# Large transfers issued from ScalarE's queue, and thirteen more attention chunks turned by DMA, in a layer kernel on one core

## What is computed

```python
xn = _layernorm(x, axis=-1)
# attention: one head, causal, with a linear bias on the distance
scores = einsum('bqe,bke->bqk', xn @ W_qk, xn) * SCALE + (kpos - qpos) * alibi_slope[0]
s = softmax(where(causal, scores, -inf)) @ (xn @ W_v.T)
# mixture of experts: 8 experts, 512 slots each, the best expert of a token alone
probs = softmax(xf @ Wr); eidx = argmax(probs); rank = place of the token in its expert
h = maximum(xe @ W1[e], 0); ye = (h @ W2[e]) * p_tok       # xe: the rows sent to expert e
x = x + s * _silu(y)
```

## Time and profile before

| | |
|---|---|
| median of 3 runs | 438.6 us (438.42 to 440.61) |
| the profiled execution, own time | 441.75 us |
| its span | 440.0 us |
| PE busy | 420.4 us, 96% |
| DVE busy | 322.4 us, 73% |
| ACT busy | 222.7 us, 51% |
| POOL busy | 228.3 us, 52% |
| DMA | 76.01 MB, mean 173 GB/s |

### The profile page before, as it was taken

The page is one execution under the profiler, slowest core; times in us unless marked ns, Lnnn a source line. Parts: engine busy times, 40 slices in busy tenths (PEclk is TensorE's granted clock), DMA queues, the critical chain, the costliest instruction groups (busy, mean ns, idle before and its releaser), DMA issues.

```text
span 440.0 us, 8367 instructions
## 1 busy us (share of the span) xinstructions
PE 420.4 (96%) x3015; PEld 288.6 (66%) x3015; DVE 322.4 (73%) x838; ACT 222.7 (51%) x444; POOL 228.3 (52%) x353
## 2 busy tenths in 40 slices
PE   6899999998999899999989999999999999999996
PEld 2667576756668676766666666666666666665666
DVE  5989778988888478778747787979796967424553
ACT  3755454452657146545424555545455545454551
POOL 3257851826544826056102566575757576757530
PEclk9999999999999999999999999999999999999999
DMA  7996898366945634266866577676888873234840
GB/s 238 294 294 151 277 295 191 74 130 163 279 90 111 139 115 117 57 216 153 120 96 232 165 245 226 205 250 176 281 156 280 179 206 98 90 120 113 159 98 31
DMA packets 104280, 76.01 MB, mean 173 GB/s; under 512 B 73263, under 2 KB 98108, under 8 KB 102192
## 3 DMA queue, kind: packets, MB, share of 16 engines
q1 hardware_dynamic: 92976, 53.11, 47.3%
q0 software_dynamic: 5824, 16.74, 12.9%
q10 hardware_dynamic: 5440, 5.64, 3.9%
HBM read 31.33 MB, written 28.58 MB: 136 GB/s over the span
## 4 chain that ended last, share of the span: by engine, by line
PE 64%; DVE 13%; DMA 11%; issue 4%; ACT 4%; POOL 1%; SPq 1%; another core or an unknown queue 0%; ACTq 0%; POOLq 0%; DVEq 0%
PE bank L1419 18%; PE bank L1421 18%; PE bank L1420 17%; DMA xg<-in_x 4%; DMA pT<-p_rows 3%; PE bank L1510 3%; DVE sc L1012 3%; PE bank L1513 3%; PE bank L1512 3%; PE bank L1491 2%; ACT sc L1269 2%; DVE p_rows L1033 2%; DMA rows<-xg 1%; DMA slots<-xnr,slot_idx 1%; DMA xeT<-slots 1%
## 5 line engine op out<-in xcount | busy, mean ns | idle before, releaser
L1510 PE MATMUL bank<-v_h,pT 128*128 128x257 f16 x272 | 74.7, 274 | 3.2 <-DMA pT<-p_rows 3.2
L1513 PE MATMUL bank<-v_h,pT 128*128 128x257 f16 x272 | 74.1, 272 | 0.0
L1512 PE MATMUL bank<-v_l,pT 128*128 128x256 f16 x272 | 73.7, 271 | 0.0
L1296 ACT ACTIVATE hid_h<-bank 128x512 f16<-128x512 f32 x64 | 38.1, 596 | 67.7 <-PE bank L1421 59.8
L1102 DVE SCALAR_TENSOR_TENSOR hid_l<-bank,hid_h 128x512 f16<-128x512 f32 x64 | 44.0, 688 | 38.0 <-ACT hid_h L1296 33.7
L1421 PE MATMUL bank<-w_h,hid_l 128*128 128x256 f16 x256 | 69.8, 273 | 0.0
L1419 PE MATMUL bank<-w_h,hid_h 128*128 128x256 f16 x256 | 69.8, 273 | 0.0
L1420 PE MATMUL bank<-w_l,hid_h 128*128 128x256 f16 x256 | 69.8, 273 | 0.0
L1012 DVE CUSTOM_DVE_ANT_0 sc<-bank,bias,score_mul 128x512 f32<-128x512 f32 (+2 forms) x80 | 52.9, 664 | 9.1 <-PE bank L1421 9.0
L1419 PE MATMUL bank<-xT,qT_h 128*128 128x512 f16 (+3 forms) x160 | 55.0, 347 | 3.1 <-DVE cmin L1012 1.7
L1285 ACT ACTIVATE pT<-bank 128x512 f16<-128x512 f32 (+3 forms) x50 | 24.6, 494 | 60.3 <-PE bank L1491 50.9
(11 more groups left out here) (198 smaller groups left out, 919.9 us busy)
## 6 DMA issues: line engine op xcount, KB each, us to landing
raw<-in_w_e SPq DMA_DIRECT2D x5, 2048.0 KB
sc<-in_w_e SPq DMA_DIRECT2D x3, 2048.0 KB
slots<-empty ACTq DMA_DIRECT2D x1, 4224.0 KB, 18.7
gates<-gate SPq DMA_DIRECT2D x8, 512.0 KB
out<-xg SPq DMA_DIRECT2D x7, 512.0 KB
rows<-xg SPq DMA_DIRECT2D x7, 512.0 KB, 7.2
rows<-so SPq DMA_DIRECT2D x7, 512.0 KB
xg<-in_x SPq DMA_DIRECT2D x6, 512.0 KB, 4.4
```

The lines of the kernel that those rows point to most:

```text
L1296: a_.activation(hid_h[:, f % HB, :], sc_ps[f % 2][:, :], ACT.Relu).then_inc(h_hi, 1)
L1510: pe.matmul(pv_ps[t % 2][:, 0:D + 1], p_h, v_h[:, at, q, 0:D + 1], start=kb == 0, stop=False)
L1512: pe.matmul(pv_ps[t % 2][:, 0:D], p_h, v_l[:, at, q, :], start=False, stop=False)
L1513: last = pe.matmul(pv_ps[t % 2][:, 0:D + 1], p_l, v_h[:, at, q, 0:D + 1], start=False, stop=kb == t % NT)
```

## The change

- Three buffers `p_rows` instead of two, the third in two blocks of `hid_h`, which the experts fill later.
- Thirteen more chunks by DMA: chunk 0 of tiles 4 to 7 and of 12 to 14; in the second sequence chunk 0 of 20, 21, 22, chunks 0 and 1 of 23, and chunk 0 of 27. `pT_in` is one semaphore per parity of the tile and chunk.
- `group_out`, `group_in`, `group_s` from group 1 or 2 on and the two weight loads of the main loop are issued from ScalarE, at the end of a step given by a table.
- A group's four turns are placed one by one after chunk turns (`turns_after`): groups 2 and 3 still after tiles 3 and 6, group 4 in tile 11, 5 in 15, 6 in 16, 7 in 21 and 22.
- Units of group 7: values in tile 23's first two steps, its rank at the end of tile 24 instead of the first step of 25. The second expert's rows are asked for after the loop.

```diff
-        p_rows = [sb(f"p_rows{k}", [P, GT, 2, P], F16) for k in range(2)]
+        p_rows = [sb(f"p_rows{k}", [P, GT, 2, P], F16) for k in range(NX - 1)]
+        p_rows += [hid_h[:, HB - 2:HB, :].rearrange("p f t -> p (f t)").rearrange("p (b h t) -> p b h t", b=GT, h=2)]
...
-            if t in (REST - 1, TILES - 1):
+            if chunk_blocks(t, c) < GT:
                 return False
-            if chunks(t) == 4:
-                return c == 1 if t == NT - 1 else c in ((1, 2) if t < NT else (0, 1, 2))
-            return chunks(t) == 3 and c < 2
+            if t < NT:
+                return c == 1 if t == NT - 1 else c in {2: (0,), 3: (0, 1), 4: (0, 1, 2)}.get(chunks(t), ())
+            return c in {REST - 1: (0,), TILES - 1: ()}.get(t, range(chunks(t)) if t >= NT + GT else ())
...
-                   REST - 5: [VAL, VAL + 1] * last,
-                   REST - 4: [VAL + 2, VAL + 3] * first + [PICK] * (c == 1),
-                   REST - 3: [RANK] * first,
+                   REST - 5: [VAL, VAL + 1] * first + [VAL + 2, VAL + 3] * (c == 1),
+                   REST - 4: [PICK] * (c == 1) + [RANK] * last,
...
+        def turns_after(t, c):
+
+            if t in (3, 6):
+                return [(t // 3 + 1, j) for j in range(GT) if last_step(t, c)]
+            if t == 11:
+                return [(4, j) for j in range(GT) if min(j, 2) == c]
+            if t in (NT - 1, NT):
+                return [(t - 10, c)]
+            if t in (REST - 7, REST - 6) and c < 2:
+                return [(LATE, (t - REST + 7) * 2 + c)]
+            return []
+
...
-        SECOND_LOAD = 23
+        FIRST_LOAD, SECOND_LOAD = (6, 0), (23, 1)
+        OUT_AT = {(4, 0): 2, (8, 0): 3, (10, 0): 4, (12, 0): 5, (17, 0): 6}
+        IN_AT = {(5, 1): 2, (9, 0): 3, (11, 1): 4, (13, 2): 5}
+        S_AT = {(6, 1): 0, (9, 2): 1, (13, 0): 2, (18, 0): 3, (21, 1): 4, (25, 1): 5}
...
                 for c in steps(t):
                     if by_dma(t, c):
                         chunk_turn(t, c)
...
+                    for g, j in turns_after(t, c):
+                        turn(g, j)
...
+                    if dma_no(t, c) >= NX:
+                        b, m = in_rows[dma_no(t, c) - NX]
+                        act.wait_ge(pT_in[b % 2][m], landed(b, m))
...
                     for g, n in units_after(t, c):
                         if n == PICK:
                             chance(g)
+                    transfers(t, c)
...
-                    pe.wait_ge(pT_in[i % 2], i // 2 * 16 + 16)
+                    pe.wait_ge(pT_in[t % 2][c], landed(t, c))
```

More of the change, by code:

```diff
@@ L303, in layer_kernel @@
         pT_lo = sem("pT_lo")
-        pT_in = [sem(f"pT_in{k}") for k in range(2)]
+        pT_in = [[sem(f"pT_in{k}_{c}") for c in range(NG)] for k in range(2)]
         pv_full = sem("pv_full")
@@ L374, in dma_no, with landed @@
             return chunk_no(t, c) - turn_no(t, c)
+        in_rows = [(t, c) for t in range(TILES) for c in range(chunks(t)) if by_dma(t, c)]
+        def landed(t, c):
+            return sum(by_dma(k, c) for k in range(t % 2, t + 1, 2)) * 16
         def chunk_cols(t, c):
@@ L499, in spread, with turn @@
                 sp.dma_start(wall[:, :], tops[e, 0:2 * P].partition_broadcast(P)).then_inc(w_spread, 16)
-            def turn(g):
+            def turn(g, j):
                 at = key_slot(g // NG, g % NG)
@@ L506, in turn @@
                     sp.wait_ge(score_full, chunk_no(NT, 0))
-                for j in range(GT):
-                    sp.wait_ge(xn_lo, rows_to(g))
-                    sp.dma_start_transpose(xT[:, at, j, :, :], halves[g % NX][:, j, :]).then_inc(xT_in[g % NX], 16)
+                sp.wait_ge(xn_lo, rows_to(g))
+                sp.dma_start_transpose(xT[:, at, j, :, :], halves[g % NX][:, j, :]).then_inc(xT_in[g % NX], 16)
             def rows_of(g):
@@ L565, in _ @@
             rows_of(0)
+            group_out(1)
             for t in range(REST):
[L567 to L574, removed]
                 if t == 1:
+                    group_in(1)
                     rows_of(1)
-                if t == 5:
-                    sp.dma_start(raw[:, :, :], w_k[0]).then_inc(w_in[1], 16)
-                if t == SPLIT_TILE[NG + 1]:
-                    group_out(NG + 1)
                 for c in steps(t):
@@ L598, in _ @@
                     next_rows(0)
-                    next_rows(1)
+            next_rows(1)
             spread(1)
@@ L1353, in _, with group_out, group_in, group_s @@
                 unit(0, n)
+            def group_out(g):
+                k, n = g % 2, (g // 2 + 1) * 16
+                act.wait_ge(x_in[k], n)
+                act.dma_start(out_g[g], xg[k][:, :, :]).then_inc(out_first[k], 16)
+                act.dma_start(rows_g[g][:, :, 0:D], xg[k][:, :, :]).then_inc(rows_x[k], 16)
+            def group_in(g):
+                k, n = g % 2, (g // 2 + 1) * 16
+                act.wait_ge(xn_made, made_to(g))
+                act.wait_ge(out_first[k], n)
+                act.wait_ge(rows_x[k], n)
+                act.dma_start(xg[k][:, :, :], x_g[g + 2]).then_inc(x_in[k], 16)
+            def group_s(g):
+                act.wait_ge(s_made, g * GT + GT)
+                act.dma_start(rows_g[g][:, :, D:2 * D], so[g % 2][:, :, :]).then_inc(rows_s[g % 2], 16)
+            def transfers(t, c):
+                if (t, c) in OUT_AT:
+                    group_out(OUT_AT[t, c])
+                if (t, c) in IN_AT:
+                    group_in(IN_AT[t, c])
+                if (t, c) in S_AT:
+                    group_s(S_AT[t, c])
+                if (t, c) == FIRST_LOAD:
+                    act.dma_start(raw[:, :, :], w_k[0]).then_inc(w_in[1], 16)
+                if (t, c) == SECOND_LOAD:
+                    act.wait_ge(w_lo, 2 * PIECES)
+                    act.dma_start(raw[:, :, :], w_k[1]).then_inc(w_in[1], 16)
             def tile(t):
```

20 lines of the change are left out of this document (4 added, 16 removed).

## The result

| | before | after |
|---|---|---|
| median | 438.51 us (437.89 to 440.61, 4 runs) | **465.91 us** (463.42 to 466.87, 4 runs) |
| ratio | | 1.061, 95% interval 1.056 to 1.066 |
| profiled execution, own time | 441.75 us | 466.84 us |
| its span | 440.0 us | 465.0 us |
| mean granted clock | 1.00 | 0.978 |

The sign was right, the size was not: 27.4 us slower where 3.9 were forecast, and far outside the range. Lines have moved: the score matmuls are L1459 to L1461, the values L1549, L1551 and L1552, the transposes L1531, ScalarE's high half L1291, VectorE's low half L1039, SP's chunk turn L575 and group turn L532.

A forecast was written before the change was run, and what follows sets the result against it. PE, busy 96% of the span, was taken as the bound. Removed transposes (-5.7) and the other gains, against new waits and lost clock, summed to +3.9 on 438.6: 442.5 us, range 435.5 to 446.5.

The forecast's parts named there:

- This is the term that decides.: Tile 4: chunk (4, 0) queues on SP behind group 2's four turns, so PE waits +7.9 us (7.5 to 9.2).
- -1.3 for the hole at 44.98: Tile 4: PE's old hole of 1.28 us vanishes because DVE reads scores during the long wait, -1.3 us.
- Tile 7, +3.7: Chunk (7, 0) queues on SP behind group 3's turns, so PE waits +3.7 us (2.5 to 5).
- The clock, +2.2 once: After tile 4's long wait PE runs at half clock for a while, charged once at +2.2 us (0 to 2.2).
- SP's shorter list, -3.8: Middle tiles: late chunk turns at 97.22 and 141.02 mended and plain transfers no longer holding DVE's x, -3.8 us.
- +2.0 for DVE's pace and `gate`: Stretch 100 to 150: DVE partly paces PE and the late weight spread makes it wait, so +2.0 us not realised.
- Second sequence, +2.4: Waits for (21, 0), 1.2 us, and for (20, 0), (22, 0) and group 7's last turn, 1.2 together.
- -0.8 for counts and -1.5 for the expert's rows: Group 7's new unit order removes the wait for counts, -0.8, and brings the first expert's rows earlier, -1.5 us.
- The last tiles, -1.2: Last four tiles: a third buffer ends ACT's waits and closes PE's holes of 0.92 and 0.3, -1.2 us.
- ScalarE's issues, 0 up to +2: ScalarE's twenty-two new issues cost 0, or up to +2 us if a wait holds exponentials back.
- the shared DMA engines: Rival, 7%: ScalarE's transfers slow chunk turns to 4.45 us, so SP's relief of 3.8 goes; +5.7, 444.3 us.
- The rival with the clock falling twice: Rival, 6%: ScalarE is held back or the clock falls twice, +3.9 + 2.2 + 2, 446.7 us.

The follow-up runs named there:

- e3: Changed kernel with every transfer that had gone to ScalarE issued from SP at the same steps; 462.46 us, ratio 1.053.
- e11: Changed kernel with chunk 0 of tiles 4 and 7 back on PE, tiles 5 and 6 still by DMA; 453.47 us, ratio 1.030.
- e10: Changed kernel with unneeded matmuls in front of the waits for (4, 0) and (7, 0); 459.89 us, ratio 1.050.
- e1: Changed kernel with chunk 0 of tiles 4 to 7 back on PE's transposes; 445.75 us, ratio 1.015.
- e2: Changed kernel with the old choice of chunks by DMA; queues, three buffers and order stay as changed; 441.73 us, ratio 1.007.
- e6: e2 with the units of group 7 back in their old order; 440.33 us, ratio 1.004.
- e7: Changed kernel with chunk 0 of tiles 12 to 14 as the only added chunks; 441.76 us, ratio 1.004.
- e13: e1 with the second load of 2 MB issued four steps earlier, at the end of step (22, 1); 443.18 us, ratio 1.011.
- e12: e8 with chunk 0 of tiles 12 to 14 by DMA as well, everything on SP as before; 439.22 us, ratio 0.999.
- e15: e8 with chunks (11, 0) and (15, 1) turned by PE; 435.66 us, ratio 0.993.
- e8: Kernel before with only the third buffer `p_rows` added; 438.41 us, ratio 0.997.
- e14: e11 with the read of x for group 2's slot issued at the end of step (6, 0) instead of (5, 1); 451.78 us, ratio 1.028.
- e5: Changed kernel with turns of (4, 0) and (7, 0) ahead of the group turns, group 2's transfers to out and rows a tile later; 461.89 us, ratio 1.053.

## Why the prediction was wrong

- **"This is the term that decides."** Right in place and mechanism, and too small: 10.65 us of wait instead of 7.9. The step that failed is "they take SP to 44.36". It took the issue time of group 2's turns from the earlier trace rows, where no group transfer ran beside them (the last had landed at 36.4). After the change SP began them at 39.60 instead of 38.76 and was through at 47.1. The last link held: the turn landed 3.18 after its issue. In e3 the step came out nearly as written: issued at 44.42, PE waiting 8.5.
- **-1.3 for the hole at 44.98**: no such hole follows the wait. It holds.
- **Tile 7, +3.7**: 4.88. The group's turns took 5.85 us instead of 5.16. The turn of (7, 0) itself took 3.7. "Chunks (5, 0) and (6, 0) are free": true in the changed kernel, where PE is late, and e11 shows that it is so for no other reason.
- **The clock, +2.2 once**: 6.5 in three places. "Nothing for the wait of 3.7" failed, and the clock fell even behind a wait of 2.60 at 197.67. The page cited from the Trainium skill, "TensorE: Matmul & The Clock Gate", section on HAM oscillation, was right to warn, and e10 shows it by a run. The argument from the start's matmuls gave a price of the right size for one fall (2.2 against 2.5, 2.3 and 1.7); what was missed is how many there would be.
- **SP's shorter list, -3.8**: it came out the other way. With the +2.0 beside it the stretch was to give 1.8 net. By PE's waits it lost 2.5: 4.0 us for turned chunks where it had been 3.2, and 2.8 for score banks where it had been 1.1. (The 6.9 and 2.5 us of idling by stretch overstate this: the stretch before starts at 100, inside the wait of 1.82 that ends at 100.48.) "Both places are mended by the new order" took the order for the time. At (15, 1) the wait is gone. At (11, 0) the order did what it should: the low half was ready at 110.50 and SP issued the turn at 110.53. With 3.2 us to its landing it would have been there at 113.7, and PE came at 115.33. But the turn took 7.8 us, beside a read of 512 KB that ScalarE issued at 111.03 and that took 6.9:

```profile
L575 SPq DMA_TRANSPOSE pT<-p_rows x1: 2211/2211/2211, 110.5 to 110.5; - x1
...
DMA to landing us min/median/max: 7.8/7.8/7.8
```

- **+2.0 for DVE's pace and `gate`**: this came. The spread was late, and DVE waited 4.63 us for it:

```profile
129.77 0.42 DVE L1079 TENSOR_REDUCE wtop<-gate 128x2 f32<-128x256 f32 x1 [4.63 <-DMA gate<-tops]
```

  PE's waits for score banks follow it: 0.95 at 135.77, 0.49 at 142.17, 0.88 at 148.46, where the kernel before has one of 0.64. DVE waits 4.1 to 5.3 us for `gate` in e1, e2, e6, e7 and e13 as well, whatever their chunks, and under 1 in e12 and e15, which have SP's order of before; so this is the new order's doing. That the waits for score banks come of it is likely and not shown, as no run moved the spread alone. DVE's own work did not pace the stretch: e15 has PE full there with DVE busy 40.69, more than in any stretch above.
- **Second sequence, +2.4**: 2.60 + 2.81 + 0.80 = 6.2 us of waits, and 1.7 of clock. The turn of (21, 0) took 4.6 us instead of 3.1, with a transfer of ScalarE's issued 0.95 behind it. Chunk (23, 1) was not seen at all; its turn took 7.4 us beside the load of 2 MB.
- **-0.8 for counts and -1.5 for the expert's rows**: the second came (1.8), the first was replaced by 1.6 for `v_l`, so that a gain of 0.8 became a loss of 0.8.
- **The last tiles, -1.2**: 1.4 in e8. In the changed kernel one wait of 1.35 for a chunk turn came in there instead, so most of it was given back.
- **ScalarE's issues, 0 up to +2**: e2 has one of 1.94 us, which accounts for 0.7 us at most.

Added up against the profiled spans, the misses are: tile 4 2.8, tile 7 1.2, the clock 4.3, the middle 4.3, the second sequence 3.8, the counts 1.6, the last tiles 1.6, the expert's rows -0.3, together 19.3 of the 21.1 us between +3.9 and +25.0. The wait of 0.9 for `xT` and 0.9 of PE's busy time are the rest. All but the last of the named terms were too low, and no one of them is the bulk.

Two mistakes lie under most of these. The forecast gave 7% to "the shared DMA engines", and sized it by taking back a gain: turns slowed to 4.45. The traces show 3.7 to 8.3 us where such a turn lands beside a plain transfer, and 1.9 to 3.5 us for an issue that takes 1.27 alone. This rival was not an alternative to the forecast; it came on top of it. The Trainium skill, "DMA: Bandwidth & Descriptors", section "Issuing engines are not separate DMA queues", says that such transfers interleave on the same engines and that a second issuer saves issue time only. The runs agree, and go further: here even the issue time of the first queue grew. And the forecast's count of falls of the clock was one, for want of a look at which of its own waits were above the only harmless one it knew, 1.8 us. The rival with the clock falling twice (6%) had the direction, at 446.7.

Neither of the two conditions under which the forecast called itself wrong came about: the longest wait in tiles 4 to 8 was 10.65, not under 5, and PE made up nothing before the experts, which began 25.8 us later than before. Both conditions guard against too small a cost, none against too large a one. The looser signs did better. PE's waits for pT were to be 10 to 13 us in all and were 27.1; no wait over 0.5 was allowed at the two mended places, and (11, 0) alone waited 3.00. Those that came: 100 transposes, DVE's wait for `gate`, and no wait of ACT for a buffer in the last tiles.

**Open.** What in a plain transfer slows a turn (its bytes, its packets or its place in an engine's queue) was not tried. e13 and e14 brought back less time than their waits were long, and neither gain is clear of the noise; where the rest went was not followed. What the new order costs without new chunks (e2, some 3 us) was not taken apart. The kernel with all thirteen chunks and every plain transfer placed clear of them was not built, and e5 shows why that is no small edit.

## What to carry to other kernels

Price a queued DMA by two durations, alone and beside what will be in flight then, and look up both: moving a transfer to another engine's queue takes its issue off the first queue and leaves its bytes beside the same turns. Before handing work from a full engine to a queue, write down for each piece when its input is ready, what stands ahead of it in the queue and when its reader comes; a piece with less than that slack is cheaper where it was. Here 0.44 us of PE bought waits of 2.6 to 10.7 in five places, and giving two such pieces back made the kernel before, with its third buffer, faster by 1.8 us (by the ratios of e15 and e8) to 2.8 (by their medians). And price a wait of TensorE twice, once for itself and once for the clock, which here fell behind some waits of 2.6 us and more and not behind others.

## What was not expected of the hardware

- A transposing DMA of 128x8x128 or 128x4x128 holds SP for 1.2 to 1.3 us when alone, and for up to 3.50 while plain transfers of ScalarE's queue are in flight.
- The same chunk turn lands 3.1 to 3.2 us after its issue alone, 4.9 beside transfers of 512 KB issued 3 us ahead of it, 7.65 and 7.8 beside one issued 0.62 and 0.50 us behind it, and 7.4 beside one of 2 MB.
- The clock fell behind a wait of 10.65 us (half from 45.09, 5.3 us before the wait ended, to 55.33), of 4.88 (75.81 to 82.64) and of 2.60 (from 198.69, 1.0 us after PE had gone on, to 202.10), but not behind the 3.00 at 118.33 or the 2.81 at 221.10; in e1 it did fall behind a wait of 2.8 for the same chunk, and in e10's trace not behind the same 2.60. Executions of one kernel differ too: the twelve of e6 have mean granted clocks from 0.992 to 1.000. No sharp limit shows. Matmuls in the wait kept it up.
